# A fused adaLN block on one core: another order of its front, and every second compression weight split on GpSimd

## What is computed

```python
mod = (silu(c) @ wmod).reshape(2, 6, 1, 512)          # sa, ca, ga, sb, cb, gb
ga = (2 * (ga >= 0) - 1) * maximum(abs(ga), 0.25)     # gb likewise
h = layernorm(x) * (1 + ca) + sa
q = rmsnorm(rope(h @ Wq_c @ Wq_up)) * q_norm_w        # 16 heads of 128
k = rmsnorm(rope(h @ Wk)) * k_norm_w;  v = h @ Wv     # one key and value head
ck = rmsnorm(h.reshape(2, 64, 16 * 512) @ W_comp) * k_norm_w
ao = softmax attention over a window of 128 keys + over the 64 compressed keys ck
x = x + ga * (grouped(ao) @ Wg).reshape(...) @ Wo
x = x + gb * ffn(layernorm(x) * (1 + cb) + sb)        # 8-bit weights, 1408 wide
```

## Time and profile before

| | us |
|---|---|
| median of 3 runs | 1054.21 (1052.88 to 1054.54) |
| the profiled execution's own time | 1053.55 |
| its span in the trace | 1051.5 |
| of which the front on PE, to its last matmul | 198.4 |
| PE busy over the span | 944.2 (90%) |
| DVE, ACT, POOL busy | 677.7, 563.4, 558.3 |

### The profile page before, as it was taken

One profiled execution on the slowest core, in us unless ns is written; L12 is line 12 of the kernel. 1 busy time (PEld: TensorE's weight loads), 2 busy tenths in 40 slices (PEclk: granted clock), 3 DMA queues, 4 the chain that ended last, 5 costly groups with the idle time before them and its releaser, 6 DMA issues. The chain is left out here.

```text
span 1051.5 us, 16048 instructions
## 1 busy us (share of the span) xinstructions
PE 944.2 (90%) x4782; PEld 786.5 (75%) x4782; DVE 677.7 (64%) x1260; ACT 563.4 (54%) x1554; POOL 558.3 (53%) x760
## 2 busy tenths in 40 slices
PE   5776889669999999999999999999848999999996
PEld 5676758457888888888778888888636777878784
DVE  1764355558888888888888888888748543242312
ACT  1563342147787777777777777777332322424221
POOL 0264000068888888888888888888303222221222
PEclk9898888869999999999999999999969999999999
DMA  7547741230312214122140231420081010020101
GB/s 242 171 161 255 286 174 61 80 98 29 126 36 97 78 43 135 30 91 90 41 138 26 62 121 41 138 66 11 11 319 61 1 44 37 1 80 1 41 0 42
DMA packets 52594, 93.66 MB, mean 89 GB/s; under 512 B 9904, under 2 KB 29360, under 8 KB 49712
## 3 DMA queue, kind: packets, MB, share of 16 engines
q1 hardware_dynamic: 41904, 64.52, 19.2%
q10 hardware_dynamic: 10624, 28.26, 7.6%
HBM read 75.33 MB, written 26.08 MB: 96 GB/s over the span
## 5 line engine op out<-in xcount | busy, mean ns | idle before, releaser
L926 PE MATMUL banks<-fold,aoT 128*128 128x512 f32 x768 | 194.1, 402 | 1.4 <-DVE aoT L1107 1.4
L1464 PE MATMUL banks<-hT,w_hi 128*128 128x512 f32 x704 | 172.8, 398 | 14.4 <-DVE w_hi L1513 12.6
L1464 PEld LDWEIGHTS banks<-hT,w_hi 128*128 128x128 f32 x704 | 133.1, 191 | 44.4 <-issue 12.6
L926 PEld LDWEIGHTS banks<-fold,aoT 128*128 128x128 f32 x768 | 140.7, 190 | 29.5 <-DVE aoT L1107 1.9
L1605 POOL TENSOR_TENSOR gus<-arena,gus 128x512 fp32r<-128x512 f32 x44 | 59.4, 1352 | 194.1 <-ACT gus L1507 194.1
L926 PE MATMUL banks<-k_st,qT 128*128 128x320 f32 (+6 forms) x768 | 123.5, 310 | 0.0
L1573 DVE SCALAR_TENSOR_TENSOR arena<-banks,sg,arena 128x512 f32<-128x512 f32 x44 | 33.0, 750 | 123.0 <-ACT arena L1502 123.0
L926 PEld LDWEIGHTS banks<-k_st,qT 128*128 128x128 f32 x768 | 109.8, 192 | 0.2
L1502 ACT ACTIVATE arena<-banks,sg 128x512 f32<-128x512 f32 x44 | 30.2, 687 | 137.1 <-PE banks L1464 137.1
L1431 PE MATMUL banks<-w_hi,gus 128*128 128x512 f32 x352 | 91.0, 399 | 10.8 <-POOL gus L1605 8.6
L926 PE MATMUL banks<-pp,v_st 128*128 128x512 f32 x360 | 99.5, 410 | 0.0
(11 more groups left out here) (184 smaller groups left out, 2012.4 us busy)
## 6 DMA issues: line engine op xcount, KB each, us to landing
arena<-in_wq_blocks ACTq DMA_DIRECT2D x8, 1056.0 KB, 4.9
wq_words<-in_wq_blocks ACTq DMA_DIRECT2D x8, 1056.0 KB, 7.0
w_lo<-wq_words SPq DMA_DIRECT2D x11, 768.0 KB, 13.8
go_raw<-in_w_go SPq DMA_DIRECT2D x16, 512.0 KB, 7.1
arena<-in_L_attn_h SPq DMA_DIRECT2D x16, 256.0 KB, 8.5
comp_raw<-in_w_comp SPq DMA_DIRECT2D x16, 256.0 KB, 5.2
v_parts<-v_out ACTq DMA_DIRECT2D x4, 1024.0 KB, 4.5
k_st<-k_parts SPq DMA_DIRECT2D x32, 128.0 KB, 2.6
```

Of the source, the lines that this page charges most:

```text
L926: last = pe.matmul(out, lhs[a], rhs[b], start=start and q == 0 and u == 0, stop=stop and q == n - 1 and u == 2)
L1464: last = pe.matmul(GU[2 * (n % 2) + w][:], parts[a][:, h, cols], hT[:, c % 2, x, k], start=(k == 0 and q == 0), stop=(k == KC - 1 and q == ...
```

## The change

The code of the front is put in another order, and some work moves between engines:

- SP loads x of chunk 0 ahead of sections 0 and 1, takes over the q/k/v weights from ACT's queue, and loads sections 3 and 4 early, into `mod_cols`, which lies where `comp_w` and what follows it will be. The rope table, the mask table and the zero stores go from the head of ACT's list to behind its chunk 0.
- PE's start becomes: columns of section 0, transpose(0), columns of section 1, columns of section 3, query(0), transpose(1), columns of section 4, key/value(0). `modT2` is written by ACT ahead of its query/key/value of chunk 0.
- The semaphore `stored` is split in `q_stored` and `v_stored`, and the q store moves up, behind the copy of v.
- `W_comp` pieces 5, 7, 9, 11, 13 and 15 are split on POOL (`ON_POOL`); ACT and DVE keep 4, 6, 8, 10, 12, 14. Piece 4 on ACT moves ahead of the last value and key stores. The last key on PE stands behind piece 4 instead of piece 3.
- Gate rows: both batches share one set of 128 rows (64 each), so 4 matmuls instead of 8 for a section. They stand behind piece 3 and piece 11 instead of between fold steps; ACT copies the result to `gates`, and DVE's `gate_steps` work on that copy behind fold weights 6 and 10.
- The four first `go_raw` loads wait for the last key transpose; the wait for the stores moves to ACT, ahead of "go high" 0.
- Fold groups 0 and 2 use banks 4 to 7, groups 1 and 3 banks 0 to 3, and a group waits for the fold low of the group two before it. "Fold high" of a group stands after "go high" 7, 11 and 15 instead of 4, 8 and 12.

```diff
+ON_POOL = [0, 1, 2, 3, 5, 7, 9, 11, 13, 15]
+ON_ACT = [4, 6, 8, 10, 12, 14]
...
+            if m - RING in ON_ACT:
+                sp.wait_ge(comp_lo, ON_ACT.index(m - RING) + 1)
             elif m >= RING:
-                sp.wait_ge(comp_early, m - RING + 1)
+                sp.wait_ge(comp_early, ON_POOL.index(m - RING) + 1)
...
+        load_x(0)
         sp.dma_start(first_two[:, 0], wmod[:, 0]).then_inc(shift_in, 16)
         sp.dma_start(first_two[:, 1], wmod[:, 1]).then_inc(scale_in, 16)
-        load_x(0)
+        sp.dma_start(raw_qkv[:], W_qkv).then_inc(w_in, 16)
         load_x(1)
+        for n in range(2):
+            sp.dma_start(mod_cols[:, n], wmod[:, 3 + n]).then_inc(cols_in[n], 16)
         load_x(2)
         sp.wait_ge(mod_mm, 1)
         for m in range(RING // 2):
             load_comp(m)
         load_x(3)
-        for m in range(RING // 2, RING + EARLY_SPLITS):
+        for m in range(RING // 2, RING):
             load_comp(m)
         sp.wait_ge(hT_mm, CHUNKS - 1)
         sp.dma_start(mod_two[:, 0], wmod[:, 2]).then_inc(rows_in, 16)
...
+        for m in range(RING, RING + EARLY_SPLITS - 1):
             load_comp(m)
         sp.wait_ge(hT_mm, CHUNKS)
         sp.dma_start(mod_two[:, 1], wmod[:, 5]).then_inc(tail_in, 16)
-        sp.wait_ge(zero_stored, 16 * BATCH)
-        sp.wait_ge(stored, STORES * CHUNKS)
-        sp.wait_ge(k_stored, 16 * CHUNKS)
+        for m in range(RING + EARLY_SPLITS - 1, M):
+            load_comp(m)
+        sp.wait_ge(kT_mm, CHUNKS)
         for n in range(4):
             load_go(n)
-        sp.wait_ge(comp_lo, M - EARLY_SPLITS)
+        sp.wait_ge(comp_lo, len(ON_ACT))
...
         sp.dma_start(raw_up[:], Wq_up).then_inc(up_in, 16)
-        sp.wait_ge(comp_mm, M)
-        sp.dma_start(mod_more[:], wmod[:, 3:5]).then_inc(cols_in, 16)
-        for n in range(4, 8):
+        for n in range(4, 10):
...
-        act.dma_start(raw_qkv[:], W_qkv).then_inc(w_in, 16)
...
-        act.dma_start(rope_all[:], table[:, K_ROPE:K_ROPE + TPB * P]).then_inc(rope_in, 16)
-        act.dma_start(kons[:], table[:, 0:K_PERSIST]).then_inc(rope_in, 16)
-
-        act.wait_ge(zeroed, 1)
-        for b in range(BATCH):
-            act.dma_start(k_parts[b * (TPB + 1)], zeros[:].bitcast(F32)).then_inc(zero_stored, 16)
...
             if c:
-                act.wait_ge(stored, STORES * c)
+                act.wait_ge(q_stored, 16 * c)
...
+            store_query(c)
             act.wait_ge(v_copied, c + 1)
+            if c:
+                act.wait_ge(v_stored, 16 * c)
...
-        def store_query_value(c):
-            tiles = slice(c * CHUNK, (c + 1) * CHUNK)
+        def store_query(c):
             act.wait_ge(q_lo, c + 1)
-            act.dma_start(q_parts[tiles].rearrange("t p a n -> p t a n"), q_out[:].bitcast(F32)).then_inc(stored, 16)
+            act.dma_start(q_parts[c * CHUNK:(c + 1) * CHUNK].rearrange("t p a n -> p t a n"), q_out[:].bitcast(F32)
+                          ).then_inc(q_stored, 16)
+
...
             if i < CHUNKS:
                 channels(i, i // (CHUNKS // BATCH))
             if i == 0:
+                act.dma_start(rope_all[:], table[:, K_ROPE:K_ROPE + TPB * P]).then_inc(rope_in, 16)
+                act.dma_start(kons[:], table[:, 0:K_PERSIST]).then_inc(rope_in, 16)
+                for b in range(BATCH):
+                    act.dma_start(k_parts[b * (TPB + 1)], zeros[:].bitcast(F32)).then_inc(zero_stored, 16)
                 act.wait_ge(sink_steps, 1)
                 act.activation(sink_e[:], sink_e[:], ACT.Exp).then_inc(sink_steps, 1)
+            if i == 1:
+                act.wait_ge(cols_mm, 2)
+                act.activation(modT2[:, 0:KC], bank[7][:, 4 * KC:6 * KC].rearrange("p (k b) -> p k b", b=BATCH), ACT.Copy)
+                act.activation(modT2[:, KC:2 * KC], bank[7][:, 6 * KC:8 * KC].rearrange("p (k b) -> p k b", b=BATCH),
+                               ACT.Identity, bias=1.0).then_inc(cols_done, 1)
             if i >= 1:
                 query_key_value(i - 1, (i - 1) // (CHUNKS // BATCH))
             if i >= 2:
                 key(i - 2)
+            if i == CHUNKS:
+                comp(EARLY_SPLITS)
             if i >= 1:
-                store_query_value(i - 1)
+                store_value(i - 1)
...
+        def gate_row(n):
+            act.wait_ge(gate_mm, n + 1)
+            act.activation(gates[:, n], bank[4][:], ACT.Copy).then_inc(gate_out, 1)
+
+        for m in range(EARLY_SPLITS + 2, M):
+            if m in ON_ACT:
+                comp(m)
+            if m == LAST_KEY + 3:
+                gate_row(0)
                 key(CHUNKS - 1)
-            elif m == EARLY_SPLITS + 1:
+            elif m == LAST_KEY + 4:
                 store_key(CHUNKS - 1, BATCH - 1)
+            elif m == M - 4:
+                act.wait_ge(zero_stored, 16 * BATCH)
+                act.wait_ge(q_stored, 16 * CHUNKS)
+                act.wait_ge(v_stored, 16 * CHUNKS)
+                act.wait_ge(k_stored, 16 * CHUNKS)
+            elif m == M - 1:
+                gate_row(1)
             if m >= M - 4:
                 go_high(m - M + 4)
...
+        go_high(4)
...
+            if n % 4 == 3:
                 fold_high(n // 4 - 1)
-            if n == 9:
...
+            if m in ON_ACT:
+                comp(m)
+            if m == LAST_KEY + 3:
                 key(CHUNKS - 1)
             if m >= M - 4:
...
+            elif n == 6:
+                dve.wait_ge(gate_out, 1)
+                gate_steps(dve, gates[:, 0], sign, mag, ga, gate_step)
+            elif n == 10:
+                dve.wait_ge(gate_out, 2)
+                gate_steps(dve, gates[:, 1], sign, mag, row, row_step)
+            elif n == 14:
+                dve.wait_ge(sd_in, 16)
+                for b in range(BATCH):
+                    dve.tensor_tensor(row[:, b], row[:, b], sdrow, ALU.mult)
+            if n % 4 == 3:
                 fold_low(n // 4 - 1)
...
+            pool.wait_ge(comp_in[m % RING], 16 * (m // RING) + 16)
+            if m >= SPLITS:
+                pool.wait_ge(comp_mm, m - SPLITS + 1)
...
-            if i == 0:
+            if i == 1:
+                pool.wait_ge(cols_mm, 2)
+            if 1 <= i < EARLY_SPLITS:
+                comp(i - 1)
+            if i == 1:
                 pool.wait_ge(rope_in, 32)
             if i >= 1:
                 key_value(i - 1, (i - 1) // (CHUNKS // BATCH))
-            if i < EARLY_SPLITS:
+            if i == EARLY_SPLITS - 1:
                 comp(i)
+        for m in ON_POOL[EARLY_SPLITS:]:
+            comp(m)
...
+        pe.wait_ge(shift_in, 16)
+        columns(0, first_two[:, 0])
         pe.wait_ge(table_in, 16)
-        for i in range(CHUNKS + 1):
+        transpose(0)
+        pe.wait_ge(scale_in, 16)
+        columns(1, first_two[:, 1]).then_inc(mod_mm, 1)
+        pe.wait_ge(mod_done, 2)
+        pe.wait_ge(cols_in[0], 16)
+        columns(2, mod_cols[:, 0]).then_inc(cols_mm, 1)
+        query(0)
+        transpose(1)
+        pe.wait_ge(cols_in[1], 16)
+        columns(3, mod_cols[:, 1]).then_inc(cols_mm, 1)
+        key_value(0)
+        for i in range(2, CHUNKS + 1):
             if i < CHUNKS:
                 transpose(i)
-            if i >= 1:
-                query_key_value(i - 1)
-            if i >= 2:
-                key(i - 2)
+            query(i - 1)
+            key_value(i - 1)
+            key(i - 2)
 
...
-                pe.wait_ge(q_lo, CHUNKS)
                 pe.wait_ge(k_scaled, CHUNKS)
                 pe.wait_ge(v_copied, CHUNKS)
                 pe.wait_ge(k_lo, CHUNKS)
+                pe.wait_ge(gate_out, 2)
...
                 if i == 0 and g >= 2:
-                    pe.wait_ge(f_lo, HG * (g - 1) + f + 1)
+                    pe.wait_ge(f_lo, HG * (g - 2) + f + 1)
...
+        def gate_rows(n, arrived):
+            pe.wait_ge(arrived, 16)
+            for k in range(KC):
+                last = pe.matmul(bank[4][:], silu_rows[:, k], mod_two[:, n, k], start=(k == 0), stop=(k == KC - 1))
+            last.then_inc(gate_mm, 1)
+
+        pe.wait_ge(rows_done, 1)
         for m in range(M):
             comp(m)
-            if m == SPLITS - 1:
+            if m == EARLY_SPLITS - 1:
+                pe.wait_ge(q_lo, CHUNKS)
+                gate_rows(0, rows_in)
+            elif m == LAST_KEY:
                 key(CHUNKS - 1)
+            elif m == M - 5:
+                pe.wait_ge(gate_out, 1)
+                gate_rows(1, tail_in)
...
-        for n in range(3, 8):
+        for n in range(3, STEPS):
             fold_step(n)
...
-    return 0 if g else 4
+    return 0 if g % 2 else 4
...
-        last = act.activation(silu_rows[:, b], csil[:, :, b:b + 1].broadcast_to([P, KC, P]), ACT.Copy)
+        last = act.activation(silu_rows[:, :, b * SHARE:(b + 1) * SHARE], csil[:, :, b:b + 1].broadcast_to([P, KC, SHARE]),
+                              ACT.Copy)
...
+        own = slice(b * SHARE, (b + 1) * SHARE)
+        for share in range(BATCH):
```

(1 more changed line is left out.)

181 lines of the change are left out of this document (75 added, 106 removed).

## The result

The changed kernel takes 1029.9 us (median of four runs, 1024.8 to 1032.46), beside 1054.38 for the kernel before on the same chip: a ratio of 0.976, interval 0.9726 to 0.9795. The sign was right, the size was not: 1018 was forecast with a range that ended at 1028. The profiled execution took 1029.34 for a span of 1027.6. The chips differ (the medians of the kernel before lie between 1051.94 and 1054.42), so two versions from different chips are better compared by their ratios, and a difference of less than about 3 us between two medians of four is not shown by them.

The account below looks back on a forecast made before the run. PE, busy for 90% of the span, was taken as the bound. Start +0.6, chunks -1.2, compression -9.3 and fold -26.2 sum to -36.1: 1053.55 becomes 1017.4, and the median, 0.7 above, 1018 us; range 1012 to 1028.

Parts of the forecast that it names:

- The fold: From the compression's end to PE's last fold matmul: 76.4 us falls to about 50, -26.2, with 3.5 lost to DVE.
- The start: Up to the end of key/value 0: 50.0 us against 49.4, +0.6, bounds -1 and +8.
- about the same sum [of bytes], so I take 9.6: Start: PE waits 9.6 us for section 0, against 9.28 before, as about equal bytes must land first.
- its bound of 10.5: Start: upper limit in us for section 0's arrival, from 2.2 MB to land against 1.9.
- Rival 1: Start: the clock stays low because twice as many column records stand there; +6 to +8, 1025 us, chance 0.15.
- The chunks: From key/value 0 to the end of key/value 3: 37.7 us shortened by 1.2, between -2 and 0.
- PE's order is the same as before from here: Chunks: PE's list is unchanged, while POOL's new order brings z of chunk 3 some 1.3 us earlier.
- The early query store: Chunks: standing ahead of `v_out` on ACT, it holds it until DVE's q low, eating part of the gain in chunk 1.
- The compression: From key/value 3 to the fold's start: 34.9 us falls to 25.6, -9.3, bounds -11 and -4.
- the key store issued at 13.5 lands by about 18.5: Compression, us after key/value 3: the last key store lands in time for piece 14, ready at 22.7.
- rival 2: Compression still paced by stores or POOL, ending about 30 us behind key/value 3; +4.5, 1022 us, chance 0.12.
- The Trainium skill's rule: Compression: shared-port locking could put POOL's pieces behind DVE subtractions, some 4 us over pieces 5 to 11; set aside.

Follow-up runs that it names:

- e9: The changed kernel with section 0 issued first on SP and x of chunk 0 loaded on ACT's queue; 1031.47 us, ratio 0.9801.
- e1: The changed kernel with section 0's load ahead of x of chunk 0 on SP's queue; 1028.88 us, ratio 0.9755.
- e10: The changed kernel with e2's start, the first fold weights loaded behind the last key store, and POOL splitting only the first four pieces; 1021.36 us, ratio 0.9709.
- e14: e11 with fold weights 0 and 1 loaded ahead of the last key store and POOL splitting every second piece again; 1020.93 us, ratio 0.969.
- e4: The changed kernel with the first four fold weight loads waiting for the last key store, as before; 1022.86 us, ratio 0.9725.
- e6: The changed kernel with POOL splitting only the first four compression pieces, ACT and DVE the rest; 1025.23 us, ratio 0.9712.
- e2: The changed kernel with the old load order, weights on ACT's queue, and columns 0 and 1 ahead of transpose 0; 1027.33 us, ratio 0.9761.
- e11: e10 with chunk 0's keys stored by SP instead of ACT; 1019.4 us, ratio 0.9687.
- e16: e15 with POOL splitting only the first four pieces; 1019.11 us, ratio 0.9689.
- e3: The changed kernel with the query store back behind the chunk's keys and values on ACT; 1027.6 us, ratio 0.9747.
- e15: e14 with the loads of fold weights 0 and 1 moved ahead of the last compression pieces; 1018.01 us, ratio 0.9662.

## Why the prediction was wrong, by its own steps

**The fold (-26.2)** was right: 48.8 measured, 50.2 forecast. The wait ahead of step 7 measured 2.25 against 2.0, the gate steps 4.7 against 4.8; behind the second gate and the fold lows only 0.5 each were left to wait. Three quarters of the gain forecast (26.2 of 36.1) and more than the whole gain measured are here.

**The start (+0.6, measured +6.0).** The step that failed is "about the same sum [of bytes], so I take 9.6". The sum did not set the time: the first 6 us of loads moved 0.87 MB instead of 1.79, and section 0 came at 13.68. The weights' leaving ACT's queue is one part of it, as e9's rates, with large loads on both queues again, suggest. The other part is the order: x went out ahead of section 0 and held its issue to 4.42, and e1, with section 0 first on the same queue, has it at 7.78. The 2.2 MB of the bound had moved by about 12.2, by after's rates in the stretches from 2 to 14 us (75, 113, 247, 259, 361 and 438 GB/s), and section 1 and the weights, issued behind section 0, shared the rest of the way. That is 4.1 of the 5.4; its bound of 10.5 was worked out from bytes alone. Another 1.6 is key/value 0, taken at 5.91 and measured at 7.48: the columns ahead of it ran fast, as forecast, though at 3.63 and not 2.9 (the 11 records in a microsecond of the earlier trace rows take in those cut by the stretch's ends; 32 records in 3.63 are 8.8 in one), and the clock then fell under the key/value, for a reason that stays open (e9, e10 and e14). Rival 1 had a low clock, but in the columns. The slow pace of columns 1, taken over from the earlier trace rows, held in this execution and not in e4 and e6, so that the same code can end its start near 52. e1 and e9 show two orders of the loads that don't mend the new start, e2 that it was not needed: moving only columns 2 and 3 ends the start at 51.3.

**The chunks (-1.2, measured +2.6).** The step "PE's order is the same as before from here" with z of chunk 3 earlier was right, and e11 to e16 show its 36.4. The step that failed is a term put at nothing: what a DMA issue on ACT costs if it stands ahead of the channel copies, 2.9 to 4.4 us of the stage with the long issue (39.3 to 40.8 against 36.4), 1.1 with the short one. The trace of before had a row of a long one, 2.22 at 82.37, which I passed over since nothing waited for it there. The early query store, whose part I did name, is not it (e3).

**The compression (-9.3, measured -3.7).** The step that failed is "the key store issued at 13.5 lands by about 18.5". It took 10.4 us, as the fold weights, which the change brings forward to the same moment, went out from 0.6 us ahead of it and beside it. This is rival 2 by its first cause; its end at X + 30 came out at X + 31.2, and it should have had the larger chance, since the earlier trace rows already had a key store of 5.6 beside other loads. With the store and the weights apart (e15) the store takes 4.8 us, about the 5 of that step, and the stage 26.3, 0.7 above the forecast, so the rest of that chain stands.

The Trainium skill's rule on DVE and GpSimd from the page "SBUF — State Buffer", section "Who interferes with whom", was weighed at some 4 us and set aside. POOL's six pieces took 12.7 us from the first copy to the last subtraction (104.35 to 117.09), where six of 1.98 make 11.9: 0.8 more, of which 0.20 is a wait for PE. Three records are longer by 0.2 to 0.5, those that run beside a subtraction of DVE's, and DVE's own subtraction at 109.09 takes 1.57 instead of 0.69, which is what ends PE's wait of 1.22 at 110.72. The trace agrees with the rule in kind, on both engines; the size was about 1 us on each and not 4, and PE's later wait of 3.46 for piece 14, behind the key store, took it in. The 1.28 that the prediction gives `v_less` alone stands in no line of the earlier trace rows; the trace after has it (96.98).

What stays open: why one DMA issue on ACT is long in eight of these kernels and short in two, why the same columns run at either pace in the start, and what takes the clock down under key/value 0. No run here settles them.

## What to carry to other kernels

Before two transfers are brought forward, look at what else is in flight then: a load that nobody waits for yet, issued beside a store on which the chain hangs, cost 3.4 us here. Work out early loads by when each is issued, on which queue and at what rate, not by bytes alone: a load behind four small ones went out 2.6 us later. And when a wait or an edit shows no gain, look whether it is hidden behind another: POOL's share was worth nothing in the kernel before, less than nothing in the changed one, and 2.6 us of the stage once the store was out of its way, though the medians show only 1.1 of it, within their noise.

## What the runs showed of the hardware

- The 512 KB key store took 10.4 us from issue to release beside four loads of 512 KB issued from 0.6 us ahead of it on the other queue, and about 3.6 without them (e4).
- The issue of one 512 KB store on ACT took 0.38 us in two kernels and 2.0 to 2.3 in eight, though the chunks' code differs little or not at all between them.
- With four loads of 256 KB at the head of SP's queue the core moved 113 GB/s from 4 to 6 us, with one of 1 MB there 287 (e1), with large loads on two queues 292 to 360 (before, e9).
- A wait of PE of 2.1 to 2.2 us within the compression's matmuls was followed by 3 to 7 us at a granted clock of 0.50 in six kernels of six, two waits of 1.2 in the same place were not in nine of ten (e4 is the tenth). It is not a rule: 2.11 did no harm in the kernel before.
- The pace can be low at a granted clock of 1.00. In the first line PE does 6 matmuls of 512 columns in two busy microseconds, and transposes and the last of them in the next:

```profile
40.00:42.00 2.00, 2.00 (x6) 1.52 (x6) 0.60 (x2) 0.00 (x0) 1.20 (x2) 1.00 0.00 0
42.00:44.00 2.00, 2.00 (x16) 1.83 (x15) 1.31 (x3) 0.00 (x0) 0.00 (x0) 1.00 0.02 4
```

In e4 the same query shows the same 6 matmuls between 36 and 38 us, at a granted clock of 0.50. Columns and transposes of the first 30 us are as slow at 1.00 in the kernel before too, so the granted clock alone doesn't price a step there; the length of its records does.
